# SyncE issues the first attention's query and key stacks, where GpSimd issued them

## The reference

```python
q = (x @ Wq.T + bq).reshape(8, 512, 16, 8).transpose(0, 2, 1, 3)   # 16 heads of 8
k, v likewise
a1 = softmax(q[:, :8] @ k[:, :8]^T * 8 ** -0.5) @ v[:, :8]
a2 = softmax(q[:, 8:] @ k[:, 8:]^T * 8 ** -0.5) @ v[:, 8:]
out = concatenate([a1 - lv * a2, a2]) @ Wp.T + bp      # lv: a scalar from the four lambda vectors
```

## Time and profile before

| | |
|---|---|
| median of 3 runs | 1486.77 us (1484.62 to 1487.56) |
| the profiled execution, its time | 1496.64 us |
| its span in the trace | 1495.1 us |
| first attention | 0 to about 440 us |
| busy, PE / DVE / ACT / POOL | 1438.5 / 1074.0 / 950.1 / 744.3 us |

### The profile page before, as it was taken

The page is one execution under the profiler, slowest core; times in us unless marked ns, Lnnn a source line. Parts: engine busy times, 40 slices in busy tenths (PEclk is TensorE's granted clock), DMA queues, the critical chain, the costliest instruction groups (busy, mean ns, idle before and its releaser), DMA issues.

```text
span 1495.1 us, 26269 instructions
## 1 busy us (share of the span) xinstructions
PE 1438.5 (96%) x8801; PEld 854.5 (57%) x8801; DVE 1074.0 (72%) x3430; ACT 950.1 (64%) x2448; POOL 744.3 (50%) x1260
## 2 busy tenths in 40 slices
PE   4999999999989999999999999999999999999999
PEld 2434443444437889974565565656565565655666
DVE  5899999999953677647667777777768777674433
ACT  4588888887874333436767777676767767674221
POOL 7434556655554653535636455463636544343322
PEclk9999999999999999999999999999999999999999
DMA  7366655456434565730000000000000000021331
GB/s 136 63 156 134 141 143 147 104 111 150 120 118 149 184 215 183 257 114 15 15 1 14 3 7 11 1 15 2 15 2 9 7 1 2 1 51 37 71 77 51
DMA packets 70601, 113.39 MB, mean 76 GB/s; under 512 B 18858, under 2 KB 35115, under 8 KB 70459
## 3 DMA queue, kind: packets, MB, share of 16 engines
q0 software_dynamic: 33104, 61.73, 17.0%
q1 hardware_dynamic: 36928, 49.19, 11.1%
q10 hardware_dynamic: 434, 0.79, 0.2%
HBM read 71.86 MB, written 39.91 MB: 75 GB/s over the span
## 4 chain that ended last, share of the span: by engine, by line
PE 79%; DVE 10%; ACT 5%; issue 2%; POOL 1%; DMA 1%; ACTq 0%; DVEq 0%; POOLq 0%
PE pS L1396 10%; PE bank L1429 9%; PE bank L1409 8%; PE bank L1240 6%; PE pS L1211 4%; DVE mx L1836 4%; PE bank L1438 4%; PE bank L1381 4%; PE pS L1315 4%; PE bank L1366 4%; PE bank L1329 3%; PE bank L1377 3%; PE pS L1316 3%; PE bank L1477 3%; PE bank L1231 3%
## 5 line engine op out<-in xcount | busy, mean ns | idle before, releaser
L2540 POOL TENSOR_SCALAR ar<-ar,rd 128x512 f32<-128x512 f32 (+3 forms) x512 | 268.2, 537 | 319.0 <-DVE rd L2271 317.1
L1836 DVE TENSOR_REDUCE mx<-pS 128x1 f32<-128x512 f32 x512 | 326.6, 678 | 19.7 <-PE pS L1211 16.2
L1656 ACT ACTIVATE ar<-ar,nm 128x512 f32<-128x512 f32 (+3 forms) x512 | 285.9, 560 | 77.3 <-DVE nm L2262 76.2
L2262 DVE CUSTOM_DVE_ANT_0 ar<-pS,maskf 128x512 f32<-128x512 f32 (+3 forms) x512 | 227.5, 482 | 7.5 <-PE pS L1396 5.7
L1566 ACT ACTIVATE ar<-bank 128x512 f32<-128x512 f32 x342 | 194.2, 598 | 48.6 <-PE bank L1231 41.7
L1409 PE MATMUL bank<-identr,all_r 128*128 128x128 f32 x1280 | 211.7, 287 | 6.0 <-DVE ar L2278 3.9
L1211 PE MATMUL pS<-all_r 64*128 64x512 f32 x512 | 205.9, 478 | 5.6 <-DVE mx L1836 4.7
L1409 PEld LDWEIGHTS bank<-identr,all_r 128*128 128x128 f32 x1280 | 134.4, 140 | 109.7 <-issue 85.6
L1666 ACT COPY ar<-bank 128x512 f32<-128x512 f32 (+3 forms) x256 | 107.1, 418 | 107.3 <-PE bank L1409 104.6
L1396 PE MATMUL pS<-ar 64*128 64x512 f32 (+3 forms) x1024 | 172.9, 456 | 0.8 <-DVE ar L2253 0.8
L1211 PEld LDWEIGHTS pS<-all_r 64*128 64x128 f32 x512 | 85.5, 192 | 127.8 <-DVE mx L1836 102.8
(11 more groups left out here) (306 smaller groups left out, 2632.6 us busy)
## 6 DMA issues: line engine op xcount, KB each, us to landing
rows_in<-zrow SPq DMA_DIRECT2D x16, 1024.0 KB, 5.5
ar<-gd SPq DMA_DIRECT2D x16, 512.0 KB, 6.5
all_r<-dk POOLq DMA_DIRECT2D x56, 128.0 KB, 4.0
dk<-xT SPq DMA_DIRECT2D x21, 256.0 KB, 3.4
dq<-xT SPq DMA_DIRECT2D x16, 256.0 KB, 5.1
rows_out<-ar SPq DMA_DIRECT2D x32, 128.0 KB
all_r<-dq POOLq DMA_DIRECT2D x28, 144.0 KB, 3.8
all_r<-dq POOLq DMA_DIRECT2D x28, 128.0 KB, 3.4
```

What stands on the lines that cost most here:

```text
L1656: S.activation(p, p, ACT.Exp, bias=nm1[:, c:c + 1], scale=-1.0, accum_out=den1[:, c:c + 1]).then_inc(*s_e1.inc(u, a))
L1836: V.tensor_reduce(mx[Gr % 2][:, col:col + 1], bS[n % 3], AX.X, ALU.max, negate=True).then_inc(*s_mx.inc(Gr, c))
L2262: V.tensor_tensor_reduce(pr_[pi][:, 0:w], pS[u % 2][:, 512 * a:512 * a + w], maskf[:, 512 - w:512], -0.125, 3e38, ALU.add, ALU.min, accum_ ...
L2540: G.tensor_scalar(p, p, rd1[:, c + a:c + a + 1], 1.0, ALU.mult, ALU.mult).then_inc(*s_p1.inc(u, a))
```

## The change

The function `stack` moves from POOL's program to SP's, and with it 128 transfers. The schedule is as before, so on SP they stand at the places in the list where POOL had them. The waits are the same ones, now in front of SP's transfers. The destination is written as float32 and not as float32r, with the same bits.

```diff
@@ sync_program @@
+        def stack(b, m):
...
+            if b >= 2:
+                SP.wait_ge(*s_st.at(4 * b - 7 + 2 * part, 3, 3))
+            else:
+                SP.wait_ge(*s_za.at(b))
+                SP.wait_ge(*s_zp.at(b))
+            if m < 4:
+
+                SP.wait_ge(*a_dq[i].at(2 * (b // 2 + 1)))
+                SP.wait_ge(*a_zq.at(2))
+                dst, src, rows, of_ = qst[i], dq[i], 18 if n else 16, 0
+            else:
+                SP.wait_ge(*a_dk[i].at(3 * (b // 2 + 1)))
+                dst, src, rows, of_ = kst[i], dk[i], 16, 8 * n
+            heads = src.rearrange("(i a) c n -> a c i n", a=2)
+            Q.dma_start(dst[64 * a + 16 * n:64 * a + 16 * n + rows, pairs, :].bitcast(F32),
+                        heads[a][of_:of_ + rows, pairs, :]).then_inc(*sem.inc())
+
...
-        mine = {"late": late, "q": q_rows, "k": k_rows, "shift_": shift, "clear": clear,
+        mine = {"late": late, "stack": stack, "q": q_rows, "k": k_rows, "shift_": shift, "clear": clear,
@@ pool_program @@
-        def stack(b, m):
...
-            heads = src.bitcast(F32R).rearrange("(i a) c n -> a c i n", a=2)
-            G.dma_start(dst[64 * a + 16 * n:64 * a + 16 * n + rows, pairs, :],
-                        heads[a][of_:of_ + rows, pairs, :]).then_inc(*sem.inc())
-
```

More of the change, by code:

```diff
@@ L1098, in k_rows @@
             Q.dma_start(dk[i][:, 8:16, :], qkp[1][:, 1, :]).then_inc(*a_dk[i].inc())
+        def stack(b, m):
+            i, part, m = b % 2, m // 8, m % 8
+            a, n = m // 2 % 2, m % 2
+            if b:
+                sem, pairs = ((a_st, a_st_late)[part][i], slice(4 * part, 4 * part + 4))
+            else:
+                sem, pairs = (a_st[0], slice(2, 8)) if part else (a_st0, slice(0, 2))
+            if b >= 2:
[7 more added lines that the diff above has]
+                dst, src, rows, of_ = qst[i], dq[i], 18 if n else 16, 0
+            else:
+                SP.wait_ge(*a_dk[i].at(3 * (b // 2 + 1)))
[3 more added lines that the diff above has]
+                        heads[a][of_:of_ + rows, pairs, :]).then_inc(*sem.inc())
         def shift(Gr):
@@ L2550, in pool_program @@
         begin()
-        mine = {"ln_": ln, "ln2": ln2, "bias_x": bias_x, "zero": zero, "zero_more": zero_more, "consts": consts, "ones": ones, "stack": stack, "parts": parts,
+        mine = {"ln_": ln, "ln2": ln2, "bias_x": bias_x, "zero": zero, "zero_more": zero_more, "consts": consts, "ones": ones, "parts": parts,
                 "land": land, "choose": chosen, "ahead": ahead,
```

## The result

The changed kernel takes 1523.07 us (median of 4 runs, 1520.75 to 1530.89), where the kernel before takes 1487.16 (median of 4, 1484.62 to 1487.61). The ratio is 1.0255, 95% interval 1.0239 to 1.0272: slower by some 36 us. I had forecast slower by 4.

The account below looks back on a forecast made before the run. The prediction took PE, busy 96% of the span, as the bound. Its terms, -0.6 + 3.7 + 1.0 + 0 = +4.1 us, took 1486.77 to 1490.9 us; the range to hold 8 in 10 was 1485.0 to 1494.5.

Parts of the forecast that it names:

- rival D: Steady part: `land` comes late, a microsecond in each of 7 batches; 1494 to 1498 us, chance 0.06.
- Term 1: Steady part: POOL, relieved of the stacks, is no longer late with `mp` for PE; -0.6 us, ends 0 and 1.3 gain.
- Term 2: Opening: POOL's long memset comes forward and holds DVE's 8x2 instruction, so first scores come late; +3.7 us (3.3 to 4.4).
- B: Opening: DVE's 8x2 is not caught by the memset; only the second stacks come later; 1485.5 to 1488.4 us, chance 0.32.
- C: Opening: batch 1's fourth xn falls behind the long memset, ACT's exponential 5.3 us late; 1492.5 us, chance 0.08.
- Term 3: Opening: batch 0's second eight stacks go out 4.8 us later, behind batch 1's query writes; PE waits +1.0 us (0 to 1.6).
- Term 4: Steady part: stacks on SP go out ahead of POOL's `land`, whose some 3 us of slack covers the delay; 0 us.

Follow-up runs that it names:

- e3: The changed kernel with only batch 0's stacks on SP, all later ones back on POOL; 1492.59 us, ratio 1.0016 to the kernel before.
- e5: e4 with batch 0's second eight stacks issued ahead of batch 1's query writes on SP; 1487.39 us, ratio 1.0003 to the kernel before.
- e4: e3 with POOL's constants and long memset held until after DVE's lambda chain; 1489.81 us, ratio 1.0017 to the kernel before.
- e9: e4 with each 18-row transfer of batch 0's stacks split into 16 and 2 rows; 1489.0 us, ratio 1.0000 to the kernel before.
- e2: The changed kernel with only batch 0's sixteen stacks back on POOL; 1520.04 us, ratio 1.0202 to the kernel before.
- e1: The changed kernel, but from batch 1 SP waits for `land` to arrive before each half's first query stack; 1499.84 us.

## Why the prediction was right or wrong

The direction was right; the size was not, and 1523.07 lies far above my range, which ended at 1494.5, and above rival D, which ended at 1498.

- **Term 1, POOL's relief, -0.6.** The waits of L1219 of 0.47 and 0.57 us are gone, and the last one, of 1.6, is still there, as I had read. e3 and e5, with the steady stacks on POOL, can't measure the gain; under the steady loss it can't be seen.
- **Term 2, the memset that comes forward, +3.7 (3.3 to 4.4).** The mechanism was right, and the size a little under my lower end: the memset started at 16.54 against my "at about 16.7", L1839 took 4.01 us, and the first scores came 3.12 us late. e4 isolates it at 2.8 us by medians (the ratios don't show it) and 3.5 by the trace. Rivals B and C fall: the 8x2 is caught, and the four xn, at 1.28 us in place of 1.12, get through. The exclusive lock of the Trainium skill (SBUF — State Buffer, "Who interferes with whom") agrees with the row: an 8x2 stands to the memset's end as a 128x4 does.
- **Term 3, the second stacks, +1.0 (0 to 1.6).** The mechanism was right, the size not: 3.46 us after, 4.1 and 4.0 in e3 and e4. I had let the stacks land at POOL's pace of 10.7 us at most. They took longer: issued up to 37.1 us, awaited until 49.87, some 13 us. e5 shows that the late place is the cause; in e9 1.2 us of it go with the form of the 18-row transfers.
- **Term 4, the steady part on SP, 0.** This step failed. I had the mechanism in full ("ahead of POOL's `land`, not behind it"), the slack right ("some 3 us"), and the price wrong: I let a megabyte "delay these by a microsecond or two". The runs show a delay of 7.0 - 1.4 = 5.6 us for the megabyte and 1.8 for half of it, at the first place where it counts. An estimate was to be had: the stretches in the earlier trace rows move 130 to 152 GB/s at a DMA share of 0.54 to 0.62, so a megabyte takes 7 to 8 us at that rate and over 4 us at a full share, and a transfer that comes last may wait for much of it. I used the fastest landing of the stacks, 2.3 us, for a transfer that would no longer meet an idle queue. "Every batch pays the excess" then came true in substance: each of the seven batches has a wait, of 1.55 to 5.54 us.

Two things made the loss larger than the 2.6 us (5.6 less 3) per batch that my slack would leave, 18 us in seven batches, where 31.9 were lost. One is PE's clock, which I had not priced at all. Six of the waits are followed by stretches at the 1.2 GHz level, and one set of eight of L1264 (L1240 before) takes 1.93 us there (at 186.48) and 1.07 behind it (at 190.26). In e2 the sum nearly closes: 22.1 us of waits and at most 12.9 from the lower clock against 33.9 lost; in e1, 6.3 of waits and at most 2.0 against 6.8. How the 11.2 us divide between the clock and other causes was not tested by itself.

The other, by the traces, is that the lateness feeds itself: at the second wait the release is only 3.8 us behind `land`'s issue, but `land` itself goes out late. The timeline of the kernel before, around one write of the maxima:

```profile
98.35 0.54 SPq L1083 DMA_DIRECT2D dq<-xT  x1
...
103.87 0.24 PE L1219 MATMUL bank<-identr,mp 128*32 128x128 f32 x1
...
105.80 14.07 SPq L1105 DMA_DIRECT2D dm<-xT  x2
109.39 1.17 POOL L2441 DMA_DIRECT2D all_r<-dm  x2 [7.37 <-DMA dm<-xT]
```

and that of the kernel after, the same place of the program:

```profile
110.27 0.37 SPq L1135 DMA_DIRECT2D rows_in<-zrow  x1
110.74 0.53 SPq L1083 DMA_DIRECT2D dq<-xT  x1
...
113.93 0.23 PE L1243 MATMUL bank<-identr,mp 128*32 128x128 f32 x1
...
117.79 1.55 SPq L1129 DMA_DIRECT2D dm<-xT  x1
119.45 1.92 SPq L1121 DMA_DIRECT2D all_r<-dq  x4
...
123.25 1.15 POOL L2441 DMA_DIRECT2D all_r<-dm  x2 [11.17 <-DMA dm<-xT]
...
128.16 0.79 PE L1255 MATMUL pS<-all_r 64*128 64x512 f32 x1 [3.81 <-DMA all_r<-dm]
```

SP's `clear` (the first of these rows) waits for `land` by `behind_land`, and the next batch's query and key writes are queued behind it in SP's program. PE stands 10.1 us later than before here, but the query writes 12.4, so they, the input loads and `clear`'s own transfer of 1024 KB crowd closer ahead of the next write of the maxima. That write is 12.0 us later, frees POOL after 5.5 us and not after 3.6, and `land` is 13.9 us later, 3.8 more than PE's own shift. PE then waits 3.81. That the crowding delays the write is read from one place in two traces; no run changed `clear` alone. I had asked what SP's own stacks wait for and found nothing; I had not asked what a late `land` holds up on SP. What this loop is worth over all batches was not measured.

None of the eleven changed kernels is faster than the one before; e5, with only batch 0 on SP, is the nearest.

## What to carry to other kernels

Before instructions that start transfers go to another queue, list the small transfers that then come behind them and give each a landing behind the whole bulk (here up to 7.0 us with a megabyte, 3.2 with half, 1.4 with none), not the fastest landing in the trace. An idle engine that is relieved gains nothing, but what stood behind the instructions taken away comes forward: ask what it meets there. And a wait of a few us on a full PE is priced with the clock that follows it.

## What the runs showed that I had not expected

- A DVE instruction of 8x2 stood 4.01 us, to the end of POOL's memset, in place of 0.16.
- PE ran at the 1.2 GHz level in the opening of both kernels, until about 60 us before and 65 us after, though the view of before says 1.00 there: a set of eight of L1240 (L1264 after) took 1.93 and 1.94 us, and the next set 1.06 in both. A clock view is worth checking against the duration of a matmul that repeats.
- SP issued four stacks in 1.44 to 1.92 us in most rows above, against 1.98 to 2.27 on POOL, but in 3.24 us at 146.48 in e1. Why is not shown.
- Bulk ahead of `land` on POOL's queue cost less by the trace (3.8 us to the release, 9.1 in all) than on SP's (7.0 and 31.9). Whether the queue, the order of arrival at the DMA engines, POOL's later issue or the loop through `clear` makes that difference stays open.
